# Transformer block with decayed linear attention and FP4 feed-forward: running sums and one addition given to GpSimd, and a new order of steps

## What is computed

```python
mod = (silu(c) @ wmod)                 # sa, ca, ga, sb, cb, gb per batch
h = layernorm(x) * (1 + ca) + sa       # layernorm: (x - m) / sqrt(v + 1e-5)
q, k = l2norm(heads(h @ Wq)), l2norm(heads(h @ Wk)); v = heads(h @ Wv)      # 16 heads of 8
beta, fast, slow = sigmoid(h @ Wb), sigmoid(h @ Wfd + bfd), sigmoid(h @ Wsd + bsd)
# for each of the two decays: a running sum over the 1024 tokens
cs = cumsum(log(decay + 1e-6)); w = exp(cs[-1] - cs)       # the sum over all LATER tokens
M = einsum(k * beta * w, v * beta) / (w.sum() + 1e-6)       # 8 x 8 per head
flux = clip(sigmoid(silu(k * beta @ Wtf1 + btf1) @ Wtf2 + btf2), .01, .99)
o = alpha * (q @ M_fast) + (1 - alpha) * (q @ M_slow)       # alpha = .5 + .3 flux
x = x + ga * (o @ Wo)
h = layernorm(x) * (1 + cb) + sb
gate, up = fp4(h) @ fp4(w_gate).T, fp4(h) @ fp4(w_up).T
x = x + gb * (fp4(silu(gate) * up) @ fp4(w_down).T)
```

## Time and profile before

| | us |
|---|---|
| median of 3 runs | 239.03 |
| lowest, highest | 237.57, 239.46 |
| the profiled execution | 237.73 |
| its span in the profile | 236.0 |

### The profile page before, as it was taken

One profiled execution on the slowest core, in us unless ns is written; L12 is line 12 of the kernel. 1 busy time (PEld: TensorE's weight loads), 2 busy tenths in 40 slices (PEclk: granted clock), 3 DMA queues, 4 the chain that ended last, 5 costly groups with the idle time before them and its releaser, 6 DMA issues.

```text
span 236.0 us, 3611 instructions
## 1 busy us (share of the span) xinstructions
PE 198.1 (84%) x1028; PEld 146.2 (62%) x1028; DVE 180.8 (77%) x442; ACT 148.1 (63%) x330; POOL 136.4 (58%) x153
## 2 busy tenths in 40 slices
PE   0898199998999899697499999999988868569984
PEld 0543195455966587355368887876786647357873
DVE  2549945989687787988979999898998989547730
ACT  2278737799999978655885757445537535543442
POOL 6301137608793595988484797865575395475240
PEclk9999779999999999999979999999999999958999
DMA  6590000000000000000000000010001000000011
GB/s 194 123 249 1 0 0 4 0 0 0 4 1 0 0 1 3 0 0 0 1 0 3 22 22 4 0 46 0 3 22 46 3 22 22 22 3 21 26 44 44
DMA packets 11340, 5.66 MB, mean 24 GB/s; under 512 B 1653, under 2 KB 11193, under 8 KB 11321
## 3 DMA queue, kind: packets, MB, share of 16 engines
q1 hardware_dynamic: 11008, 5.31, 8.2%
q10 hardware_dynamic: 312, 0.13, 0.2%
HBM read 3.34 MB, written 2.10 MB: 23 GB/s over the span
## 4 chain that ended last, share of the span: by engine, by line
PE 24%; issue 10%; DVE 9%; POOL 8%; ACT 3%; POOLq 1%; DVEq 0%; ACTq 0%
PE pv L1098 5%; POOL q_o L450 5%; PE pa L1096 5%; PE pv L1060 3%; DVE q_x L909 2%; POOL q_r L438 2%; DVE q_am L893 2%; PE pa L1087 2%; PE pa L1119 2%; PE pg L1045 2%; PE pa L1107 2%; DVE q_r L912 1%; PE pv L1079 1%; ACT q_A L639 1%; PE pa L1069 1%
## 5 line engine op out<-in xcount | busy, mean ns | idle before, releaser
L450 POOL TENSOR_TENSOR q_o<-q_r,q_sp 128x960 f32<-128x960 f32 (+2 forms) x18 | 30.6, 1698 | 20.3 <-DVE q_r L912 15.4
L438 POOL TENSOR_TENSOR q_r<-q_x,q_rs 128x960 f32<-128x960 f32 (+2 forms) x18 | 29.7, 1652 | 15.3 <-DVE q_rs L901 15.3
L1022 PE MATMUL pa<-wcat,hT 128*128 128x496 f32 x64 | 29.6, 587 | 0.6 <-ACT hqT L645 0.5
L1096 PE MATMUL pa<-guT,hqT 128*128 128x352 f32 x64 | 26.0, 490 | 1.2 <-ACT hqT L645 1.1
L1119 PE MATMUL pa<-wdg,fqT 128*128 128x128 f32 x192 | 26.7, 275 | 0.0
L654 ACT ACTIVATE sgl<-pa 128x352 f32<-128x352 f32 x32 | 14.6, 463 | 18.4 <-PE pa L1096 16.1
L909 DVE SCALAR_TENSOR_TENSOR q_x<-q_A,q_r 128x960 f32<-128x960 f32 (+2 forms) x18 | 18.7, 1037 | 9.2 <-ACT q_A L639 9.0
L1098 PE MATMUL pv<-guT,hqT 128*128 128x352 f32 x64 | 25.1, 475 | 0.4 <-DVE oc L850 0.3
L1119 PEld LDWEIGHTS pa<-wdg,fqT 128*128 128x128 f32 x192 | 24.0, 192 | 0.0
L923 DVE TENSOR_TENSOR q_x<-sgl,pv 128x352 f32<-128x352 f32 x32 | 15.9, 516 | 7.2 <-PE pv L1098 6.1
L406 POOL TENSOR_TENSOR vs<-kvg,cw 128x256 f32<-128x256 f32 x32 | 19.2, 627 | 2.6 <-DVE cw L808 2.6
(11 more groups left out here) (144 smaller groups left out, 477.0 us busy)
## 6 DMA issues: line engine op xcount, KB each, us to landing
x_all<-in_L_attn_x_dram SPq DMA_DIRECT2D x4, 512.0 KB, 6.4
out_dram<-x_all SPq DMA_DIRECT2D x16, 128.0 KB, 1.8
wmod_sb<-in_L_wmod_dram SPq DMA_DIRECT2D x1, 384.0 KB, 4.5
wraw<-in_L_ffn_w_down_dram SPq DMA_DIRECT2D x1, 176.0 KB, 4.4
wraw<-in_L_ffn_w_gate_dram SPq DMA_DIRECT2D x1, 128.0 KB, 3.4
wraw<-in_L_ffn_w_up_dram SPq DMA_DIRECT2D x1, 128.0 KB, 3.0
wcat<-in_L_attn_Wq_dram ACTq DMA_DIRECT2D x1, 64.0 KB, 3.5
wcat<-in_L_attn_Wk_dram ACTq DMA_DIRECT2D x1, 64.0 KB, 4.4
```

Source lines behind the costliest of these rows:

```text
L438: g.tensor_tensor(blocks(q_r[:, s % 2, c]), blocks(q_x[:, s % 2, c]), spread(q_rs[:, s % 2, n]), ALU.mult)\
L450: g.tensor_tensor(blocks(q_o[:, s % 2, c]), blocks(q_r[:, s % 2, c]), spread(q_sp[:, s % 2, n]), ALU.mult)\
L1022: te.matmul(bank_a(("PP%d" % k, i))[:, 0:NCAT], hT[:, b, 2 * j + k, :], wcat[:, :], start=True, stop=True).then_inc(S["a_full"], 1)
L1096: te.matmul(bank_a(("G%d" % k, i))[:, 0:I], lhs, guT[:, 0, :], start=True, stop=True)\
```

## The change

1. GC: GpSimd first turns `lf` in place into sums over this and the later tiles, by three additions over 7, 6 and 4 tiles (a tile plus the next, plus the second next, plus the fourth next). TensorE then needs one matmul with the strict triangle (256 columns) and one with the other triangle, diagonal included (`trile`), over the next tile (224 columns). GpSimd builds `trile` at the start.
2. GE on TensorE: one matmul of 256 columns in place of eight of 32; the sum over the tiles is a new VectorE reduction in GF, from PSUM.
3. The addition of sb moves from the head of Q on VectorE (L890) to L1 on GpSimd, in place behind the multiplication.
4. The 1e-5 of both layer norms sits as a third column beside mean and variance, and a `tensor_reduce` over two columns replaces the `tensor_scalar`.
5. `x` of batch 0 comes in two loads with a semaphore each, and `x` of batch 1 is issued ahead of the five bias loads instead of behind the FFN weights.
6. O3 on GpSimd waits also for `xn2` of the pair two before. All four lists of steps are reordered.

```diff
     "gpsimd": """
-        P0:0 P0:1 GB:0 V0:0 GE:0 V1:0 V2:0 V3:0 GF:0 P0:2 GO:0 P0:3 W2:0 GB:1 O3:0 GE:1 O3:1 V0:1 V1:1 V2:1 L1:0
+        P0:0 P0:1 GC:0 GB:0 GE:0 V0:0 V1:0 V2:0 P0:2 V3:0 GF:0 W2:0 P0:3 GO:0 GO:1 GC:1 GB:1 O3:0 GE:1 O3:1 V0:1
...
     "vector": """
-        P0:0 MV:0 XN:0 XN:1 XN:2 W1:0 XN:3 PP:0 P0:1 PP:1 PP:2 GA:0 PP:3 XN:4 XN:5 GB:0 W0:0 GK:0 GF:0 GE:0 P0:2
+        P0:0 MV:0 XN:0 XN:1 P0:1 XN:2 XN:3 W1:0 XN:4 XN:5 PP:0 PP:1 PP:2 XN:6 GA:0 XN:7 PP:3 GB:0 W0:0 GK:0 PP:4
...
     "tensor": """
-        setup:0 MB:0 KW:0 PX:0 PX:1 PX:2 PP:0 PP:1 PX:3 PP:2 PP:3 GC:0 PX:4 PX:5 GE:0 PP:4 V0:0 PP:5 V1:0 V2:0
+        setup:0 MB:0 KW:0 PX:0 PX:1 PX:2 PP:0 PX:3 PP:1 PP:2 PP:3 PX:4 PX:5 PP:4 PX:6 GC:0 GE:0 PX:7 PP:5 PP:6
...
-            sp.dma_start(x_all[:, 0], x_v[0]).then_inc(S["x0"], 16)
+            for k in range(2):
+                sp.dma_start(x_all[:, 0, 4 * k:4 * k + 4], x_v[0][:, 4 * k:4 * k + 4]).then_inc(S["x0" if k == 0 else "x0b"], 16)
...
+            sp.dma_start(x_all[:, 1], x_v[1]).then_inc(S["x1"], 16)
             sp.dma_start(bias48[:, H:2 * H], bfd.partition_broadcast(P)).then_inc(S["wsm"], 16)
...
+            def GC(b):
+
+                pool.wait_ge(S["lf"], b + 1)
+                for k, d in enumerate((1, 2, 4)):
+                    if k:
+                        pool.wait_ge(S["sfx"], 3 * b + k)
+                    g.tensor_tensor(lf[:, 0:T - d, :], lf[:, 0:T - d, :], lf[:, d:T, :], ALU.add).then_inc(S["sfx"], 1)
...
             def O3(i):
                 pool.wait_ge(S["veb"], i + 1)
+                if i >= 2:
+                    pool.wait_ge(S["xn2"], 2 * i - 2)
...
+                pool.wait_ge(S["u"], i + 1)
+                h2 = q_x[:, (i + Q_NORM) % 2, QF0:QCOLS].rearrange("p (t d) -> p t d", t=2)
+                g.tensor_tensor(h2, h2, mb[:, b, 1, :].unsqueeze(1).to_broadcast([P, 2, D]), ALU.add).then_inc(S["h2"], 1)
...
-                v.tensor_scalar(rt1[:, :], t[:, 0:2 * H], 1e-6, 1.0 / FLUX_GAIN, ALU.add, ALU.mult).then_inc(S["g_free"], 1)
+                v.tensor_reduce(ws[:, :], t[:, 0:T * 2 * H].rearrange("p (t c) -> p c t", t=T), axis=AX.X, op=ALU.add)\
+                    .then_inc(S["g_free"], 1)
                 dve.wait_ge(S["g_free"], slot_g[("TOT", b)] + 1)
+                v.tensor_scalar(rt1[:, :], ws[:, :], 1e-6, 1.0 / FLUX_GAIN, ALU.add, ALU.mult).then_inc(S["rt1"], 1)
...
-                v.tensor_scalar(veb[:, r, :], mvb[:, r, :, 1], 1e-5, None, ALU.add).then_inc(S["veb"], 1)
+                v.tensor_reduce(veb[:, r, :], mvb[:, r, :, 1:3], axis=AX.X, op=ALU.add).then_inc(S["veb"], 1)
...
-                    h2 = q_x[:, r, QF0:QCOLS].rearrange("p (t d) -> p t d", t=2)
-                    dve.wait_ge(S["u"], s - Q_NORM + 1)
-                    v.tensor_tensor(h2, h2, mb[:, (s - Q_NORM) // NP_, 1, :].unsqueeze(1).to_broadcast([P, 2, D]),
-                                    ALU.add).then_inc(S["h2"], 1)
                     dve.wait_ge(S["h2"], s - Q_NORM + 1)
...
-                pe.wait_ge(S["lf"], b + 1)
+                pe.wait_ge(S["sfx"], 3 * b + 3)
                 t = bank_g(("TRI", b))[:, 0:T * 2 * H].rearrange("p (t c) -> p t c", t=T)
                 te.matmul(t, tri[:, :], lf[:, :, :], start=True, stop=False)
-                for d in range(1, T):
-                    last = te.matmul(t[:, 0:T - d, :], ones[:, :], lf[:, d:T, :], start=False, stop=(d == T - 1))
-                last.then_inc(S["g_full"], 1)
+                te.matmul(t[:, 0:T - 1, :], trile[:, :], lf[:, 1:T, :], start=False, stop=True).then_inc(S["g_full"], 1)
...
-                t = bank_g(("TOT", b))[:, 0:2 * H]
-                for n in range(T):
-                    last = te.matmul(t, ones[:, :], wexp[:, n, :], start=(n == 0), stop=(n == T - 1))
-                last.then_inc(S["g_full"], 1)
+                te.matmul(bank_g(("TOT", b))[:, 0:T * 2 * H], ones[:, :], wexp[:, :, :].rearrange("p t c -> p (t c)"),
+                          start=True, stop=True).then_inc(S["g_full"], 1)
```

More of the change, by code:

```diff
@@ new lines @@
+    "scalar": """
+        setup:0 MB:0 KW:0 PX:0 PX:1 PX:2 PP:0 PX:3 PP:1 PP:2 PP:3 GA:0 PX:4 PX:5 PP:4 W1:0 GD:0 PX:6 GS:0 PX:7
+        PP:5 GE:0 PP:6 PP:7 XN:8 XN:9 PX:8 XN:10 PX:9 PP:8 GG:0 GA:1 PP:9 XN:11 O2:0 O2:1 PX:10 GD:1 GS:1 PX:11
+        O2:2 XN:12 PP:10 L1:0 PP:11 O2:3 XN:13 PX:12 XN:14 L1:1 W3:0 L1:2 GE:1 PX:13 QA:4 PX:14 PP:12 GG:1 GA:2
+        N4:0 O2:4 QA:5 PP:13 F1:0 L1:3 O2:5 GS:2 GD:2 N4:1 QA:6 F1:1 XN:15 L1:4 O2:6 PP:14 F3:0 PX:15 L1:5 N4:2
+        QA:7 PP:15 F1:2 N4:3 F1:3 GE:2 F3:1 O2:7 QA:8 GA:3 F4:0 GG:2 N4:4 L1:6 QA:9 GD:3 F1:4 O2:8 GS:3 F3:2
+        N4:5 QA:10 L1:7 F4:1 F1:5 L1:8 O2:9 N4:6 F3:3 QA:11 F1:6 O2:10 N4:7 O2:11 L1:9 F1:7 QA:12 F3:4 F4:2
+        QA:13 F4:3 GG:3 F3:5 N4:8 GE:3 L1:10 F1:8 O2:12 F4:4 N4:9 QA:14 L1:11 O2:13 F1:9 F3:6 F4:5 N4:10 QA:15
+        L1:12 F3:7 F1:10 O2:14 N4:11 L1:13 F1:11 QA:16 F4:6 O2:15 F3:8 F4:7 N4:12 L1:14 QA:17 F3:9 F1:12 F4:8
+        N4:13 F1:13 QA:18 L1:15 F4:9 F3:10 F3:11 F4:10 N4:14 QA:19 F1:14 F3:12 F4:11 F4:12 N4:15 QA:20 F1:15
+        F3:13 QA:21 F3:14 F4:13 F4:14 F3:15 F4:15""",
@@ L157, in adaln_block_kernel @@
         ones = sb("ones", [P, P])
+        trile = sb("trile", [P, P])
+        ws = sb("ws", [P, 2 * H])
         mask = sb("mask", [P, H, DK])
@@ L311, in _ @@
             sp.dma_start(wraw[:, DOWN0:DOWN0 + I], w_down).then_inc(S["wffn"], 16)
-            for b in range(1, NB):
+            for b in range(2, NB):
                 sp.dma_start(x_all[:, b], x_v[b]).then_inc(S["x%d" % b], 16)
@@ L318, in _ @@
             sp.wait_ge(S["out"], 16 * PAIRS)
-        N_CONST = 8
+        N_CONST = 9
         @block.gpsimd
@@ L328, in _ @@
             g.memset(mask[:, :, :], 1.0).then_inc(S["pool_c"], 1)
+            g.memset(trile[:, :], 1.0).then_inc(S["pool_c"], 1)
             g.memset(rep8[:, :], 0.0).then_inc(S["pool_c"], 1)
-            pool.wait_ge(S["pool_c"], 4)
+            pool.wait_ge(S["pool_c"], 5)
             g.affine_select(out=ident[:, :], in_=ident[:, :], compare_op=ALU.not_equal, fill=1.0, base=0,
@@ L335, in _ @@
                             pattern=[[-1, P]], channel_multiplier=1).then_inc(S["const"], 1)
+            g.affine_select(out=trile[:, :], in_=trile[:, :], compare_op=ALU.is_ge, fill=0.0, base=0,
+                            pattern=[[1, P]], channel_multiplier=-1).then_inc(S["const"], 1)
             v8 = rep8[:, :].rearrange("k (h d) -> k h d", d=DK)
@@ L460, in GH @@
                                 ALU.mult).then_inc(S["wdg"], 1)
-            run = {"W2": W2, "W3": W3, "P0": P0, "GB": GB, "GE": GE, "GF": GF, "GO": GO, "GH": GH, "O3": O3, "L1": L1,
+            run = {"W2": W2, "W3": W3, "P0": P0, "GB": GB, "GC": GC, "GE": GE, "GF": GF, "GO": GO, "GH": GH, "O3": O3, "L1": L1,
                    "QR": QR, "QO": QO}
@@ L754, in P0 @@
             def P0(b):
-                dve.wait_ge(S["x%d" % b], 16)
                 r = b
                 for t in range(T):
+                    if t == 0:
+                        dve.wait_ge(S["x%d" % b], 16)
+                    elif b == 0 and t == T // 2:
+                        dve.wait_ge(S["x0b"], 16)
                     v.bn_stats(st6[:, r, t, :], x_all[:, b, t, :]).then_inc(S["bn"], 1)
@@ L764, in P0 @@
                 dve.wait_ge(S["nmean"], b + 1)
-                v.tensor_scalar(ve[:, r, :], mv[:, r, :, 1], 1e-5, None, ALU.add).then_inc(S["ve"], 1)
+                if b == 0:
+                    dve.wait_ge(S["eps"], 2)
+                v.tensor_reduce(ve[:, r, :], mv[:, r, :, 1:3], axis=AX.X, op=ALU.add).then_inc(S["ve"], 1)
             def PP(i):
```

71 lines of the change are left out of this document (32 added, 39 removed).

## The result

| | before | after |
|---|---|---|
| median of the runs | 238.3 us (4 runs) | 228.29 us (4 runs) |
| lowest, highest | 237.40, 239.46 | 228.01, 228.58 |
| span of the profiled execution | 236.0 | 226.8 |

The kernel before has one run more here than the three on which the forecast was based, hence 238.3 and not 239.03. The ratio of the medians is 0.958, 95% interval 0.952 to 0.963: 10.0 us faster, against 230.6 predicted with a range of 223 to 238. First the busy times of the profile page after the change. The kernel before had matmuls of TensorE (PE) at 198.1 us, VectorE (DVE) at 180.8 and GpSimd (POOL) at 136.4.

A forecast was written before the change was run, and what follows sets the result against it. No engine bounds the whole span: TensorE is tightest from 30 to 90 us, VectorE and TensorE to 150, VectorE to 210, then a chain. -3 + 0.5 - 1 - 3.6 - 2.3 + 1 = -8.4: span 227.6, median 230.6, range 223 to 238.

The forecast's parts named there:

- its case (226 to 235): Whole kernel: the forecast's own outcome, a median between 226 and 235 us, given a chance of 0.60.
- Start (A): Start to first value scaling: shorter GC and GE and work pulled into TensorE's idle time save 3 us.
- `cw` of batch 0 near 34 us: Sign at the start: the first value scaling, at 36.31 us before, would begin near 34 us.
- Loads (L): Loads at the start: halves of `x` save nothing, biases queued behind `x` of batch 1 cost 0.5 us (bounds 0, 3.62).
- Second batch (B): Second batch, around 58 to 65 us: 1 us saved, chosen between +0.8 for GpSimd's additions and -2.7 from TensorE.
- 90 to 150 (C): Batches 2 and 3, 90 to 150 us: TensorE saves 5.4, VectorE 3.6; the smaller counts, -3.6 us.
- the rival that foresaw it growing: Quantisation loop sets the pace, TensorE's saved 10.8 us become idle time: 237 to 240 us; chance 0.16 for 235 to 241.
- Full gain: Whole kernel: TensorE and VectorE savings both arrive, no contention: -15.8 us, median 223; chance 0.15 for 222 to 226.
- 150 to 210 (D): 150 to 210 us: VectorE bounds and saves 4.6 at most; half taken, -2.3 us, as GpSimd's addition may delay QO.
- Contention: All steps: 18.7 us more GpSimd work holds up VectorE's scales and two-input operations, +1 us (bounds 0 and 18).
- GpSimd as the bound: Where L1 and GC stand: GpSimd's added work all lands on the path, +8 us, median 247; chance 0.09 for above 241.

The follow-up runs named there:

- e11_after_again: The changed kernel itself, nothing altered, run again beside the two variants that move steps around step 14: 228.64 us, ratio 0.963 to the kernel before.
- e7_px_first: Changed kernel with PX:4 and PX:5 ahead of GA:0 in ScalarE's list, nothing else: 229.05 us, ratio 0.961 to the kernel before.
- e8_bias_first: Changed kernel with the five bias loads issued ahead of `x` of batch 1, nothing else: 229.81 us, ratio 0.963 to the kernel before.
- e9_hole: Changed kernel with L1:10 and GY:3 moved earlier on VectorE and GE:3 on ScalarE, no work changed: 224.85 us, ratio 0.942 to the kernel before.
- e1_old_order: Changed kernel (changes 1 to 5) with the four old lists of steps, GC on GpSimd put in front of GB: 244.39 us, ratio 1.025 to the kernel before.
- e12_add_alone: Old lists and old work, only the addition of sb moved to GpSimd, with the new loads and O3's wait: 241.09 us, ratio 1.009 to the kernel before.
- e2_order_alone: Changed kernel with changes 1 to 4 undone; new lists, new loads and O3's wait kept: 244.55 us, ratio 1.028 to the kernel before.

## Why the prediction was right, and where its steps were not

The time was 2.3 us under the forecast and inside its case (226 to 235). The sum gave a span of 227.6, and it was 226.8; the other 1.5 us are the 1.3 by which I put the median above the profiled execution, where it came out 0.2 below. The terms behind the sum fit less well.

- **Start (A), -3: wrong.** Measured +1.2 at `cw` of batch 0 in the first profile and -0.4 in `e11_after_again`, the same kernel; the sign "`cw` of batch 0 near 34 us" did not come, it was 37.5 and 35.9. The step that failed is "the new list also puts PX:4, PX:5, PP:4 and PX:6 ahead of GC:0, into the 5.49 us in which TensorE idles": I read TensorE's list and not ScalarE's, which makes their input after GA:0. The idle time stayed at 5.47. And where `e7_px_first` did move GC to 31.71, TensorE still stood 5.23 us and the time did not follow.
- **Loads (L), +0.5: not to be told.** ScalarE waited for the biases until 10.86 in place of 9.53, and the XN that stood at 14.80 came at 15.71 in one execution and 14.11 in the other of the same kernel. `e8_bias_first` gains nothing.
- **Second batch (B), -1: about right up to step 4.** From `cw` of batch 0 to the maxima of step 4 the difference changes by -0.8 in the first profile and by -0.9 in the second. From step 4 to step 6 (70 to 85 us) it changes by another -2.5, for which the sum had no term of its own.
- **90 to 150 (C), -3.6: right in kind, half the size.** From step 6 to step 13 the difference grows by 7.2, from 65.2 us to 58.0. The same stretch in the columns of the earlier trace rows, first before, then after:

```profile
86.90:152.10 65.20, 57.49 (x310) 43.81 (x309) 58.23 (x123) 43.22 (x86) 49.98 (x51) 0.97 0.02 5
84.80:142.80 58.00, 51.71 (x258) 36.99 (x257) 53.85 (x116) 40.00 (x85) 54.53 (x58) 1.00 0.02 6
```

TensorE's busy time falls by 5.8 us, its 5.4 of removed work and some half speed, and its idle time from 7.7 to 6.3, against the rival that foresaw it growing. VectorE's busy time falls by 4.4 and its idle time by 2.8. So the step that failed is "Both engines are tight, so the smaller counts": TensorE's whole saving arrived, as in the rival *Full gain*, and waiting went on top. The long waits for `q_o` that the new lists shortened (11.0 us before, 3.8 after) lie mostly elsewhere: only 3.2 of the 11.0 between 90 and 120, and the rest after 180.
- **150 to 210 (D), -2.3: 0 in the changed kernel, -3.0 in `e9_hole`.** From the maxima of step 13 to those of step 21 it is 70.3 us before, 70.4 after, and 208.4 - 141.1 = 67.3 with the hole closed. The saving was there, and a new wait took it. (`e9_hole` also moves 0.8 us of work to a place where VectorE waited, so not all of the 3.0 is term D.)
- **Contention, +1: the term that was mis-sized.** I spread the overlap evenly over the time, 8% of two operations a step. VectorE's work should have fallen by 7.5 (additions) + 3.4 (`veb`) + 0.3 (`ve`) - 1.8 (the total's reduction, 418 ns where I took 300, and what goes with it), so 9.4; it fell by 3.0. Of the 6.4 us between, the groups by line show 4.8 in unchanged operations: the means of `coef` went from 292 to 930 and from 284 to 388 ns, `cf` from 352 to 472, `eg` from 384 to 520, `mb_sgn` from 420 to 650. The other 1.6 are not traced; the groups sum to more than the engine's busy time in both kernels (201 against 181 us before), since consecutive instructions overlap. Overlap with GpSimd is not random: an order repeats the same neighbours. The first `coef` took 0.29 us in all four batches before and 0.56 to 1.84 in all four after, and in the kernel before eight of the eighteen scale steps took 0.51 us in place of 0.19, each ending within 0.06 us of the end of a `q_o` product. The chain paid for one pair of operations, 1.67 and 1.84 us before `oc`, and in one of the two profiled executions for the half speed behind.
- **GpSimd as the bound: did not come, with these lists.** The block maxima waited 0.5 us for the moved addition. `e1_old_order`, at 244.4, is near the 247 of that rival, but not by its mechanism alone: there the maxima wait 1.7 us for the addition (2.0 in `e12_add_alone`), and it is TensorE that waits for `q_o` and the sums.

A rule of the Trainium skill (SBUF — State Buffer, section "SBUF: two separate sides") has a VectorE operation in a two-port mode, or with two SBUF inputs where GpSimd's instruction reads SBUF, shut out for the whole of a GpSimd instruction that started first. The traces agree for GpSimd's products: 0.10 and 1.67 us for the same `nmrb`, 0.29 and 1.84 for the same `coef`, and 156 to 159 ns at every `veb` once it is a reduction. They do not agree for its power on two values: in the kernel before a `coef` of 0.29 us at 119.35 and an addition of 0.42 at 163.98 ran inside such instructions of 0.70 us (119.27 and 163.74) without waiting.

That the total came out near the forecast is luck: A and contention failed on one side and C on the other. What stays open: how the 7.2 us of C divide between work and order, since neither half alone gives them (from step 6 to step 13 `e1_old_order` takes 69.9 us and `e2_order_alone` 64.8, against 65.2 before and 58.0 after); the runs show only that each part is needed with the new lists. The loads in halves, the early `x` of batch 1 and O3's wait were never undone together or tried alone.

## What to carry to other kernels

Where every engine has a fixed list, the price of an edit is read with the list that belongs to it: the same work was 6.7 us slower with one order and 10 us faster with another. A step moved on one engine is only as early as its inputs in the lists of the others, so read all of them before counting idle time as filled. And after giving work to GpSimd, look through VectorE's small operations for one whose longest duration is many times its shortest; moving two such steps to where GpSimd is between instructions changed no work and gave 3.8 us here.
